# Exponentials of units 2 to 6 and of most logits as powers of e on GpSimd, and the steps of the units placed anew

## The reference, cut to what matters

```python
# layer 1, on x1 = layernorm(x), context rows c (77 per batch)
h    = tanh(c @ Ws [over t] + x1 @ W [over token] + b)          # 4 x 1024 x 77 x 256 values
rho  = h @ w                                                    # 4 x 1024 x 77
att  = softmax(rho + mask)                                      # over the 77 rows
w_s, b_s = tanh((att @ c) @ Wcw + bcw), tanh((att @ c) @ Wcb + bcb)
x    = x + w_s * x1 + b_s
# layer 2, on y = layernorm(x)
probs = softmax(y @ gate)                                       # over 8 experts
scores, tokens = top_k(probs of each expert, 512)
routed = scatter_add(tokens, expert(y[tokens]) * scores)
x = x + routed + (gelu(y @ Ws1 + bs1) @ Ws2 + bs2)              # shared expert
```

## Time and profile before

| | |
|---|---|
| median of 3 runs | 899.01 us |
| profiled execution, its own time | 897.72 us |
| its span (first to last instruction) | 896.0 us |
| TensorE clock granted, mean | 0.985 of full speed |
| PE busy | 803.9 us (90%) |
| ACT busy | 767.6 us (86%) |
| DVE busy | 710.4 us (79%) |
| POOL busy | 315.5 us (35%) |
| ACT, tanh L974 | 157 instructions, 520.9 us |
| ACT_TABLE_LOAD | 12: ahead of gelu 6, of att 4, of logits 1, of the first tanh 1 |

### The profile page before, as it was taken

One profiled execution on the slowest core, in us unless ns is written; L12 is line 12 of the kernel. 1 busy time (PEld: TensorE's weight loads), 2 busy tenths in 40 slices (PEclk: granted clock), 3 DMA queues, 4 the chain that ended last, 5 costly groups with the idle time before them and its releaser, 6 DMA issues.

```text
span 896.0 us, 14132 instructions
## 1 busy us (share of the span) xinstructions
PE 803.9 (90%) x5375; PEld 473.6 (53%) x5375; DVE 710.4 (79%) x1412; ACT 767.6 (86%) x600; POOL 315.5 (35%) x563
## 2 busy tenths in 40 slices
PE   7875679679998999999999999999889999999996
PEld 5321123124443444445354455545766899999986
DVE  5799889897989699988879995884887876676641
ACT  3989999999999999999999999997753677667672
POOL 3310540615544008774002740051303155554424
PEclk9999999989999999999999999999999999999999
DMA  8000000000001000200000010002101365545413
GB/s 262 22 1 0 1 1 1 1 24 1 25 1 48 1 1 3 93 2 1 24 1 1 25 48 1 24 1 105 61 24 54 115 185 141 134 105 134 135 21 41
DMA packets 32406, 41.82 MB, mean 47 GB/s; under 512 B 2365, under 2 KB 29011, under 8 KB 32339
## 3 DMA queue, kind: packets, MB, share of 16 engines
q1 hardware_dynamic: 26083, 32.49, 10.9%
q0 software_dynamic: 6144, 8.39, 5.6%
q10 hardware_dynamic: 112, 0.04, 0.0%
HBM read 28.33 MB, written 12.58 MB: 46 GB/s over the span
## 4 chain that ended last, share of the span: by engine, by line
PE 41%; ACT 36%; issue 10%; DVE 9%; POOL 2%; DMA 0%; POOLq 0%; ACTq 0%; DVEq 0%
ACT z L974 30%; PE bank L893 10%; PE bank L916 9%; PE bank L773 7%; PE bank L824 5%; DVE z L1331 5%; PE bank L809 3%; ACT z L970 2%; ACT u L1011 2%; PE bank L749 1%; PE bank L701 1%; PE bank L931 1%; PE bank L867 1%; ACT L1011 1%; DMA x_ring<-in_x_dram 0%
## 5 line engine op out<-in xcount | busy, mean ns | idle before, releaser
L974 ACT ACTIVATE z<-z 128x4096 f32<-128x4096 f32 (+5 forms) x157 | 520.9, 3363 | 6.5 <-DVE z L1331 6.2
L1331 DVE TENSOR_SCALAR z<-feat,txt_bias 128x1024 f32<-128x1024 f32 (+1 forms) x722 | 421.0, 655 | 34.6 <-PE bank L773 33.4
L773 PE MATMUL bank<-z,window 128*32 128x512 f32 x2464 | 309.0, 612 | 61.4 <-ACT z L974 60.0
L773 PEld LDWEIGHTS bank<-z,window 128*32 128x32 f32 x2464 | 70.6, 111 | 251.9 <-issue 137.0
L824 PE MATMUL bank<-ws_sb,u 128*128 128x256 f32 x512 | 128.2, 391 | 5.5 <-ACT u L1011 5.5
L824 PEld LDWEIGHTS bank<-ws_sb,u 128*128 128x128 f32 x512 | 93.3, 192 | 41.4 <-issue 19.8
L809 PE MATMUL bank<-tr,ws_s 128*128 128x512 f32 x384 | 107.5, 416 | 0.0
L893 PE MATMUL bank<-xg_s,w_s 128*128 128x512 f32 x384 | 99.6, 397 | 0.2 <-DVE xg_s L1633 0.2
L916 PEld LDWEIGHTS bank<-w_s,hid_s 128*128 128x128 f32 x672 | 86.4, 188 | 4.0
L916 PE MATMUL bank<-w_s,hid_s 128*128 128x256 f32 x672 | 88.2, 280 | 0.0
L1047 ACT ACTIVATE hid<-bank,vec 128x512 f32<-128x512 f32 x64 | 44.2, 690 | 49.4 <-PE bank L893 49.4
(11 more groups left out here) (237 smaller groups left out, 754.8 us busy)
## 6 DMA issues: line engine op xcount, KB each, us to landing
w_raw<-in_L_ffn_W_dram SPq DMA_DIRECT2D x16, 1024.0 KB, 5.6
x_ring<-in_x_dram SPq DMA_DIRECT2D x8, 512.0 KB, 7.8
xn_dram<-xn SPq DMA_DIRECT2D x8, 512.0 KB, 2.9
out_dram<-x_ring SPq DMA_DIRECT2D x8, 512.0 KB, 2.9
u<-in_L_ffn_Ws_dram SPq DMA_DIRECT2D x1, 1024.0 KB, 12.4
ws_sb<-in_L_ffn_Ws_dram SPq DMA_DIRECT2D x1, 1024.0 KB, 15.0
xg<-xn_dram,idx POOLq DMA_INDIRECT x32, 3.6
out_dram<-y,idx POOLq DMA_INDIRECT x32, 3.9
```

What stands on the lines that cost most here:

```text
L773: ins = e.matmul(sums[v][32 * r:32 * r + 32, :], window[:, c, 31 - k:63 - k], z[:, n % ZB, at_piece:at_piece + TOK], start=(v, r) not in b ...
L974: e.activation(part, part, ACT.Tanh).then_inc(signal(*step), 1)
L1331: ins = e.tensor_scalar(z[:, n % ZB, i * width:(i + 1) * width], feat_of(units, c), bias_of(units, t, c), None, ALU.add)
```

## The change

The exponentials of the attention of units 2 to 6 (`POWERS_FROM = 2`, up to but not including unit 7), and those of the logits of units 0 to 5, leave ACT. GpSimd does them in two instructions each: the argument is held between -87 and 0, and then a power is taken, with e (a column of one value, read again for each element) as base and the argument as exponent. Units 0 and 1 (attention), unit 7 (attention) and units 6 and 7 (logits) keep ACT's Exp. Seven tables of block numbers change; the other edits are the constant, the names and the waits.

```diff
+LEAST_POWER = -87.0
-TAIL_EARLY = (0, 0, 1, 4, 5, 5, 5, 4, 11, 6, 10, 12, 12, 14)
+TAIL_EARLY = (0, 0, 1, 0, 5, 5, 5, 5, 9, 5, 10, 11, 11, 14)
-TAIL_SINGLE = (-1, 0, 1, 2, 3, 5, 5, 9, 12, 10, 11, 10, 11, 13)
+TAIL_SINGLE = (-1, 0, 0, 3, 4, 5, 5, 9, 11, 9, 11, 10, 12, 13)
...
-FFN = ((8, 2.2), (34, 2.1), (13, 2.3), (36, 2.0), (13, 1.5), (26, 1.6))
+FFN = ((8, 2.2), (34, 2.0), (13, 2.3), (35, 2.1), (13, 1.7), (26, 1.6))
+POWERS_FROM = 2
...
+        exponential = "att_pow" if POWERS_FROM <= v < vb else "att_exp"
+        return [[("rho_out", v)], [("rho_turn", v)], [("att_shift", v)], [(exponential, v)], [("weigh", v)],
...
-        return [[("logits_exp", v)], [("router", v)]]
+        return [[("logits_pow", v)], [("router", v)]]
...
+            e.memset(euler[:], math.e)
...
+                elif kind in ("att_pow", "logits_pow"):
+                    v, = args
+                    x_ = (att[:, v % 2] if kind == "att_pow" else lg[:, v]).rearrange("p j n -> p (j n)")
+                    e.wait_ge(*done("att_shift" if kind == "att_pow" else "logits_shift", v))
+                    e.wait_ge(consts, CONSTS)
+                    link(e.tensor_scalar(x_, x_, 0.0, LEAST_POWER, ALU.min, ALU.max))
+                    e.wait_ge(pool_link, linked)
+                    e.tensor_tensor(x_, euler[:].broadcast_to([P, J * (R if kind == "att_pow" else E)]), x_, ALU.pow).then_inc(signal(*step), 1)
...
-                    e.wait_ge(*done("att_exp", v))
+                    e.wait_ge(*done("att_pow" if POWERS_FROM <= v < vb else "att_exp", v))
...
-                    e.wait_ge(*done("logits_exp", v))
+                    e.wait_ge(*done("logits_pow" if v < va else "logits_exp", v))
```

More of the change, by code:

```diff
@@ L1 @@
+import math
 from contextlib import ExitStack
@@ L40 @@
 PRE_LATE = (25, 27, 28, 31, 32, 32, 34, 34, 36, 35, 39)
-TAIL_EARLY = (0, 0, 1, 4, 5, 5, 5, 4, 11, 6, 10, 12, 12, 14)
+TAIL_EARLY = (0, 0, 1, 0, 5, 5, 5, 5, 9, 5, 10, 11, 11, 14)
 TAIL_FIRST = (0, 0, 1, 3, 3, 4, 6, 6, 9, 6, 11, 11, 11, 13)
-TAIL_LATE = (0, 1, 2, 3, 8, 9, 10, 9, 13, 11, 15, 16, 16, 24)
-TAIL_SINGLE = (-1, 0, 1, 2, 3, 5, 5, 9, 12, 10, 11, 10, 11, 13)
+TAIL_LATE = (0, 1, 2, 4, 8, 9, 9, 9, 13, 9, 14, 17, 16, 22)
+TAIL_SINGLE = (-1, 0, 0, 3, 4, 5, 5, 9, 11, 9, 11, 10, 12, 13)
 FFN_PLACES = (-1, 1, 2)
-FFN = ((8, 2.2), (34, 2.1), (13, 2.3), (36, 2.0), (13, 1.5), (26, 1.6))
+FFN = ((8, 2.2), (34, 2.0), (13, 2.3), (35, 2.1), (13, 1.7), (26, 1.6))
 LAG = 2
+POWERS_FROM = 2
 BY_VECTOR = ("down_end", "store_out", "load_x")
@@ L127, in tail @@
     def tail(v):
-        return [[("rho_out", v)], [("rho_turn", v)], [("att_shift", v)], [("att_exp", v)], [("weigh", v)],
+        exponential = "att_pow" if POWERS_FROM <= v < vb else "att_exp"
+        return [[("rho_out", v)], [("rho_turn", v)], [("att_shift", v)], [(exponential, v)], [("weigh", v)],
                 [("gate_in", v)], [("gates", v)], [("y_scale", v)], [("logits_shift", v)],
@@ L421, in xattn_moe_kernel @@
         bc = sb("bc", [P, 2])
+        euler = sb("euler", [P, 1])
         x_stat = sb("x_stat", [P, J, 6])
```

## The result

The changed kernel takes 1124.2 us (median of 4, 1123.0 to 1126.9), the kernel before 898.3 beside it: a ratio of 1.252 (95%: 1.2495 to 1.2544). The forecast was 890. The span of the profiled execution is 1122.1 us in place of 896.0, so its own rows have to account for 226 us.

What follows compares the result with a forecast made beforehand. ACT was taken to bound the tanh stage, 205 to 615 us: 11.1 us off it, 10.5 after DVE's missing lead, 9.0 after 1.5 for PE, POOL's lateness and tables; 899.0 becomes 890.0 us, range 886 to 910.

Steps and rivals of the forecast that it cites:

- the length of a power: On POOL: a power takes 4 us for 128 x 320 and 0.6 for 128 x 32; the step trusted least.
- 14 passes of 0.64 are 9.0 us for 320: Upper end for a power on POOL, taken from the 14 instructions of the reciprocal root in `inverse_root`.
- 12.2 us for one clamp and one power, enough for both ends: End of batch 1: time from unit 2's shift, 320.6, to its `weigh`, 332.9, hides POOL's clamp and power.
- Rival 1: A power keeps DVE's adds out until it ends, at three places: 14.3 us slower, 913; chance 0.22.
- Rival 2: Powers hold DVE up but last 2 to 3 us: 8.5 to 12.7 us back, 898 to 901; chance 0.14.
- Rival 3: No hold, powers near 9.0 and 3.2 us, `y_scale` 11.5 us late: gain 2, 897; chance 0.08.
- Rival 4: PE, busy for 95% of the tanh stage, becomes the limit: half the gain, 5.5 us, 893.5; chance 0.06.
- The work taken off ACT: Ends of batches 1 and 2 and of unit 6: 11.1 us less, 10.5 after waits, gain 9.0 after deductions.
- At the other two places I find nothing like it: End of batch 2 and unit 6: no loss from DVE lacking lead, unlike the 0.6 us at batch 1.
- The forecast's own range: Whole kernel: 886.5 to 894 us if the forecast's own account holds, rivals left out.
- The sum for POOL's block: End of batch 1: eight POOL instructions take 16.3 us from 320.6, to 336.9, making `y_scale` 1.6 us late.
- The other table changes: Steps moved by one or two blocks with the same work: priced at nothing, as PE and DVE have slack.

Runs made afterwards that it cites:

- experiment 7: Changed kernel, but the power covers only 24 of 320 attention elements and 4 of 32 logits elements, an add covering the rest: 897.4 us, ratio 1.000.
- experiment 3: Kernel before plus three 128x320 powers on GpSimd over a buffer nobody reads, behind the layernorm of units 3, 5 and 7: 911.3 us, ratio 1.016.
- experiment 9: Kernel before without the exponentials of units 2 to 6 and the logits of units 0 to 5, nothing in their place: 888.2 us, ratio 0.990.
- experiments 9 and 2: The 2: changed kernel with an add in the power's place and the seven tables of places of the kernel before: 892.2 us, ratio 0.994.
- ten passes: Changed kernel with the attention's exponentials as ten plain passes on GpSimd in place of clamp and power, logits powers kept: 926.2 us, ratio 1.032.
- experiment 4: Separate test, none of the kernel computed: GpSimd and DVE instructions one at a time, nothing beside them; power 51.36 us, multiply of the same shape 0.86.

## Why the prediction was wrong

**The step that failed is the length of a power**, "I take 4 us and 0.6", with "14 passes of 0.64 are 9.0 us for 320" as the upper end: 51.4 and 5.4 us. The price was bounded by what other instructions of this engine do, and a function inside one instruction is not bound by them. Rows of the trace gave a lower end only; the upper was a guess dressed as one, and the range of 886 to 910 followed from it.

**What lies beside it.** "12.2 us for one clamp and one power, enough for both ends" fell with it: `weigh` waited 40.06 us. The order of events was as written, POOL, `weigh`, ACT. What is not in the forecast is who stands in line: with `weigh` late, DVE's adds are late, and ACT waits for the gates and for z. With powers of 4.6 us no `weigh` waits (experiment 7), so the 12.2 us themselves were rightly read.

**Rival 1 is refuted**, and so is the rule behind it as the prediction applied it to a power. Adds keep 0.67 us beside a power; the first four took 3.40 us in place of 2.73, for one add was longer beside the clamp and one at the power's start, and two idle powers cost 0.0 us (experiment 3). The price is that of a start and not the length of the power. Rival 2 goes with it; its own sum, 8.5 to 12.7 us back against 11.1, gives 896 to 901 and not 898 to 901. **Rival 3 was the right mechanism**, no hold and powers too long for the slack; it had 0.08, and its size, 897, came from the same upper end. Its signs came: the transpose, now L707, waits up to 45.9 us for `xn`, and `y_scale` begins at 436.74, right behind the last power. But it is `weigh` that waits first. **Rival 4**, PE as the next limit at half the gain, falls with experiment 9: 9.4 us were gained and not 5.5.

**The work taken off ACT** was sized nearly right in the sum, with luck. Forecast were 3.2, 3.85 and 3.44 us at the three ends, 10.5, and 9.0 after the deduction; with nothing on POOL ACT gained 2.9, 1.6 and 3.5, and the kernel 9.4. "At the other two places I find nothing like it" was wrong for batch 2, where ACT waited 1.76 us for the gates. The loads fell to six, each 1.283 us, and ACT's busy time by 9.1. The forecast's own range, by its terms, begins at 887.5 (899.0 less 10.0 less 1.5) and not at 886.5.

**Had a power taken 4 us**, 890 would still have been wrong, by up to 7 (experiment 7, whose kernel has a third pass on POOL beside each power). The sum for POOL's block was 16.3 us from 320.6; with powers of 4.6 it was 24.5, and 21.5 in batch 2. Plain passes of 128 x 320 take up to 1.74 us beside DVE's adds, those of 128 x 32 up to 1.27, and not 0.64 or 0.23 and one add. They lengthen the adds as well, which the forecast had at 0.15 us each: 1.20 in place of 0.75 for many. Two plain passes cost 3.7 us by themselves (experiments 9 and 2: 8.0 against 4.2 us gained across the three ends). **The other table changes**, "I price them at nothing", cost up to 4 us with a cheap pass, between the medians, of which the traces show 1.1 at the three ends, and were worth 33 us with the real powers.

## What to carry over

An instruction that the trace never shows has no upper bound from its neighbours; where a change rests on one, the range must hold the case that it is ten times as long, or its price is measured alone first. Then ask when its result is read: a long instruction costs its length less the slack up to its first reader, together with all that its engine's order puts between, and nothing at all if nobody reads it soon. Where two long ones stand in line, the one that is read first goes first. And a pass moved to GpSimd beside a busy VectorE costs twice: itself, up to 1.74 us where 0.64 was reckoned, and up to half a microsecond of VectorE's add beside it.

## What the runs showed of the hardware

- `pow` on GpSimd: 160 ns for each element of a row, 51.4 us for 128 x 320, the same for 16 partitions, for constants and for data.
- A power in progress leaves DVE's adds alone; the add at its start takes 1.20 us in place of 0.75. Plain passes one after the other lengthen add after add: twelve take 10.81 and 12.11 us beside ten passes, in place of 8.04.
- Some powers end late, within 0.1 us of the end of an unbroken row of DVE's adds: 7.98 us and 10.57 for 4.6, and 16.30 for 5.4. Others of the same shapes end inside such a row at their usual length: 4.54 us with 3.9 us of adds to come, and, with ten passes, 5.59 us for 128 x 32. What decides between the two stays open.
- A plain pass of 128 x 320 on POOL takes 0.45 us with DVE's adds at rest in the changed kernel, 0.86 (multiply) and 1.02 (tensor_scalar) alone in experiment 4, and up to 1.74 beside the adds.
- DVE's RECIPROCAL takes 2.15 us for 128 x 320, 6.7 ns an element, in which a tensor_scalar of that shape takes 0.32. The row of 128 x 4, 0.18 us, does not tell. The Trainium skill ("VectorE: DVE Perf Modes", section "First, the fixed hardware budget") has it as a repeated division of 8 steps; the ratio here is 6.7.
- A mean granted clock of 0.64 in a stretch in which TensorE has 17.53 us of work in 63, and no cost of it that shows.
